# A reworked opening, another order of TensorE's attention work, and values awaited by block, in a two-layer transformer kernel

## What is computed

```python
x = layernorm(x + L0_attn(x))   # energy = x.T @ x (256 x 256), softmax over it, out = x @ attention.T
x = layernorm(x + L0_ffn(x))    # gated FFN, 896 wide, LoRA of 8 experts, top 2 by a router
x = layernorm(x + L1_attn(x))   # causal attention, 16 heads of 16, then w_o
x = layernorm(x + L1_ffn(x))    # 32 experts 96 wide, top 8 cut at a share of 0.8
```

## Time and profile before

| | |
|---|---|
| median of 3 runs | 1439.48 us (1438.6 to 1439.6) |
| the profiled execution's own time | 1448.79 us |
| its span, first to last instruction | 1447.1 us |
| PE busy | 1374.4 us (95%) |
| DVE busy | 931.0 us (64%) |
| ACT busy | 625.9 us (43%) |
| POOL busy | 247.1 us (17%) |
| mean granted TensorE clock | 0.959 of 2.4 GHz |

### The profile page before, as it was taken

How to read it: one execution, slowest core, us unless ns; L and a number is a source line. 1 busy time by engine, 2 the same in 40 slices (tenths; PEclk the granted TensorE clock), 3 DMA queues, 4 the chain that set the end, 5 groups by cost and what they waited for, 6 DMA issues and landing times.

```text
span 1447.1 us, 20119 instructions
## 1 busy us (share of the span) xinstructions
PE 1374.4 (95%) x7836; PEld 975.4 (67%) x7836; DVE 931.0 (64%) x1781; ACT 625.9 (43%) x892; POOL 247.1 (17%) x342
## 2 busy tenths in 40 slices
PE   8999899899899999999999999999999999999996
PEld 6787687687688754344344344454788888888886
DVE  3855754754755777778888888854656455665545
ACT  3323323323323323556666766647343344434432
POOL 1300200200200001022122122211112222222221
PEclk9999999999999985799999999969999999999998
DMA  7000000000000542302201500000011111111110
GB/s 296 1 0 1 0 1 1 0 1 1 22 0 1 163 163 53 77 2 41 49 2 24 67 2 2 13 12 6 19 42 45 46 54 45 44 46 54 44 63 30
DMA packets 32231, 55.40 MB, mean 38 GB/s; under 512 B 6408, under 2 KB 13320, under 8 KB 31752
## 3 DMA queue, kind: packets, MB, share of 16 engines
q1 hardware_dynamic: 30088, 53.85, 13.2%
q0 software_dynamic: 2048, 0.27, 0.1%
HBM read 43.21 MB, written 10.49 MB: 37 GB/s over the span
## 4 chain that ended last, share of the span: by engine, by line
PE 77%; DVE 14%; ACT 4%; issue 3%; DMA 1%; SPq 1%; POOL 0%; POOLq 0%; DVEq 0%; ACTq 0%
PE ps L1393 50%; PE ps L1709 9%; PE ps L1633 9%; PE ps L1687 5%; DVE mpart L1174 4%; ACT probs L833 1%; PE ps L1651 1%; PE ps L1432 1%; SPq L560 1%; DVE x2u L1134 1%; DVE x L914 1%; DMA w_raw<-in_w 1%; PE ps L1718 1%; DVE x2f L1115 1%; DVE x2f L1101 1%
## 5 line engine op out<-in xcount | busy, mean ns | idle before, releaser
L833 ACT ACTIVATE probs<-ps 128x1024 f32<-128x1024 f32 (+3 forms) x320 | 273.7, 895 | 190.4 <-PE ps L1687 189.1
L1393 PE MATMUL ps<-xtd,gu 128*128 128x512 f32 x1152 | 277.9, 395 | 3.6 <-DVE hmul L1301 3.0
L1174 DVE TENSOR_REDUCE mpart<-ps 128x1 f32<-128x512 f32 x384 | 240.1, 683 | 47.0 <-PE ps L1633 45.8
L1393 PEld LDWEIGHTS ps<-xtd,gu 128*128 128x128 f32 x1152 | 212.5, 188 | 52.6 <-issue 4.9
L1633 PE MATMUL ps<-stack 48*128 48x512 f32 (+2 forms) x832 | 206.4, 401 | 16.2 <-DVE mpart L1174 7.7
L1633 PEld LDWEIGHTS ps<-stack 48*128 48x128 f32 x832 | 108.1, 198 | 147.2 <-DVE mpart L1174 92.9
L1393 PE MATMUL ps<-ma,b 128*128 128x512 f32 x672 | 168.8, 400 | 11.2 <-DVE ma L914 7.5
L1687 PE MATMUL ps<-stack 50*128 50x512 f32 (+3 forms) x640 | 161.1, 441 | 8.7 <-ACT probs L833 4.6
L1709 PE MATMUL ps<-probs,vaug 128*32 128x512 f32 (+3 forms) x1280 | 163.6, 587 | 0.7 <-ACT usum L725 0.7
L1393 PEld LDWEIGHTS ps<-ma,b 128*128 128x128 f32 x672 | 126.6, 190 | 43.0 <-DVE ma L914 9.4
L1393 PEld LDWEIGHTS ps<-dn,hpart 128*128 128x128 f32 x1152 | 143.8, 189 | 4.2
(11 more groups left out here) (184 smaller groups left out, 1576.3 us busy)
## 6 DMA issues: line engine op xcount, KB each, us to landing
gu_raw<-in_wgu SPq DMA_DIRECT2D x48, 256.0 KB, 2.6
stack<-qk_dram SPq DMA_DIRECT2D x72, 128.0 KB, 4.0
qk_dram<-qk_out SPq DMA_DIRECT2D x16, 512.0 KB, 2.9
dn_raw<-in_wdn SPq DMA_DIRECT2D x48, 128.0 KB, 2.6
stack<-qk_dram SPq DMA_DIRECT2D x48, 64.0 KB, 2.4
x<-in_x_tm SPq DMA_DIRECT2D x4, 512.0 KB, 5.2
out<-x SPq DMA_DIRECT2D x4, 512.0 KB, 3.1
w_raw<-in_w SPq DMA_DIRECT2D x1, 1792.0 KB, 10.0
```

The source lines that it names most:

```text
L833: act.activation(probs[:, (2 * r + p) % 4, :, off:BLK], banks(bank)[:, :, off:BLK], ACT.Exp, scale=float(HD) ** -0.5).then_inc(exp_done.se ...
L1174: ins = dve.tensor_reduce(part[:, p, qt % TPB, 2 + kb:3 + kb], ps[:, bank, :], AX_X, ALU.max)
L1393: mm = pe.matmul(out, lhs(i), rhs(k), start=first and n == 1, stop=last and n == todo, **more)
```

## The change

Five things change in the opening.

1. PE gets work that nobody reads: `keep_busy(n)` issues n bf16 matmuls of 128x512 into bank 7 from a constant tile of ones that POOL writes first (`const`). Six run ahead of the energy, eight between the energy and the turning of the attention, three between that and the mixing.
2. Tile 0 of `x` has a DMA of its own (`x_first`), ahead of the other four, so that SP issues one DMA more.
3. ACT writes the high part of `w13` in two halves (`w13_hi`); of `a13` only after the exponentials of the energy.
4. DVE subtracts only the first half of `w13` ahead of the maxima; the second half and `a13` come after the copies of `att_t`, ahead of tile 0.
5. `att_t` moves into the place of a quarter of `ma`'s last low part; POOL therefore waits for the last mixing matmul before the third of its four subtractions for block 0.

In the attention `ORDER` is another string, with the same number of each letter, and the wait of `P` for the values moves from all four blocks at once to the block of the round (`v_ready`).

```diff
-    "qqTLRqNqVuuTuuuVuuTuuVMuuuquuquuuquuuSquuuVuuSuuSSuuuPuuPSuuuuSuuuPuuMuuuSuuuuSuuSuSuuuuPuuuuuuuuuuuSSuPuSSPuS"
+    "qqTLRqqNVuTuuVuuuquuqMuTuuuuuSuuSuVuuuPuuSuSuuuquuuVuuPuuMquuSSSuuSPuuuSuuuuuPuuuuuuuuuOuuSuuuSSuuPSSuuuPuuSuS"
...
-        att_t = at("att_t", [P, NC, H], F32, B_END - 11 * BLK * 4)
+        att_t = at("att_t", [P, NC, H], F32, MA + 28 * 1024)
...
+            sp_.dma_start(x[:, 0:1, :], x_tm[:, 0:1, :]).then_inc(x_first, 16)
             for b in range(NB):
-                sp_.dma_start(x[:, TPB * b:TPB * (b + 1), :], x_tm[:, TPB * b:TPB * (b + 1), :]).then_inc(x_in[b], 16)
+                t = max(TPB * b, 1)
+                sp_.dma_start(x[:, t:TPB * (b + 1), :], x_tm[:, t:TPB * (b + 1), :]).then_inc(x_in[b], 16)
...
+            pool.memset(const[:, :], 1.0).then_inc(const_ready, 1)
...
                     pool.wait_ge(*ma_hi.after((b, w, c, 1)))
+                    if (b, w, c) == (0, 1, 0):
+                        pool.wait_ge(*mix_late_ready.after(NT - 1))
...
-            weights_hi("w13", w13_raw, w13)
-            weights_hi("a13", a13_raw, a13)
+            act.wait_ge(w0_in["w13"], 16)
+            for c in range(NC):
+                copy(w13[:, 0, c], w13_raw[:, c]).then_inc(w13_hi, 1)
+            act.wait_ge(w0_in["a13"], 16)
...
+            weights_hi("a13", a13_raw, a13)
             weights_hi("b13", b13_raw, b13)
...
-            weights_lo("w13", w13_raw, w13)
-            weights_lo("a13", a13_raw, a13)
+            def w13_lo(c):
+                dve.wait_ge(w13_hi, c + 1)
+                low(w13[:, 1, c], w13_raw[:, c], w13[:, 0, c]).then_inc(w0_ready["w13"], 1)
+
+            w13_lo(0)
...
                 dve.tensor_copy(att_t[:, j, :], ps[:, 2 + j, 0:H]).then_inc(att_tsb.sem, 1)
+            w13_lo(1)
+            weights_lo("a13", a13_raw, a13)
...
+            pe.wait_ge(const_ready, 1)
+            def keep_busy(n):
+                for i in range(n):
+                    pe.matmul(ps[:, 7, :], const[:, 0:P], const[:, :], start=True, stop=True)
+
+            keep_busy(6)
+            pe.wait_ge(x_first, 16)
...
             pe.wait_ge(consts_in, 80)
+            keep_busy(8)
...
                 mm.then_inc(att_tps.sem, 1)
+            keep_busy(3)
             pe.wait_ge(xfm_in, 16)
...
                         pe.wait_ge(*out0_read.after((NB - 1, TPB - 1)))
-                        pe.wait_ge(*v_ready.after(NB - 1))
+                    if g == 0:
+                        pe.wait_ge(*v_ready.after(qb))
```

More of the change, by code:

```diff
@@ L56 @@
 ORDER = (
[L57 to L66 removed]
+    "qqTLRqqNVuTuuVuuuquuqMuTuuuuuSuuSuVuuuPuuSuSuuuquuuVuuPuuMquuSSSuuSPuuuSuuuuuPuuuuuuuuuOuuSuuuSSuuPSSuuuPuuSuS"
+    "uPuuuuSuMPuuSuSuSuPuuSPuSuSSuuPSuuPuSuSuuPuSuuuuSuPSuuuSuuSuuPuuuSSuuPuSuuuSPuuuSuuPSuuSuuSuuPuuuuPuSuSuuSuSPM"
+    "uuPSuSuSuSPuOSMuSPSuuSuPuuSuSPuuSuSuPuuSSuPSuuuSuPuuSuSPSuuPSSuSuuPuSuSuPSuSPSuMuSuPSuuuSPSuOuSuPuuSuSuPSuPuSu"
+    "uSSuPuuSuOPSuuSuuSuPuSSuPuSuPSuSuuSuMPSuSuuPuSSuuOuPuuuSuPSuuuuSSuPSSuuPuuuSPuuSSuuSPSuuuuSPSuuSuPuSuuPuSSuuSu"
+    "uPuSuuSuPuuSuuPuSuSSuPuSuPuuSSuMPSuuuSuOuPSSuuPuSSuuSuuuPSuuSPuSuuPSMuuSuSuPSuuuPuSuuSuSPuuSuSuMPuuuPuuSSuuSuS"
+    "PSuSuuPuSSuuPuuSSPuSuPuSuuSuuuuSuPSSuuPuuSSuPSSuOPuuuSuuSPSSuuuPOuuSSPSuuuSPSuSMuPuSOuSuPSSuuuuPSuuuuSuyPSuSPu"
+    "SuSuPSuuSuPuYuSSuPuSuSuuPuuuSPuuSuSuuSPuSSuuuPSuuPuSSuuuuuPuSuuSPuMSSuuPuuSuSSuOuPuSSuPuuSSuPuSuSPuuSSuuPuSSuP"
+    "uuSSuPSuuuSPSuSMuPuSuMSPSuSuPSuSuPSuSuOPuuuSSuPSuSuPuSSuuPuSuSuuPuSuuuSuPPuuSuSSuSuPSSuuPuSSuuPuSSPuuuSOPuwSOS"
+    "uuauSPuuSuSPSuPSMuSSuuuPuSuSuuPuSuuSPSuuPuSuuSPuSuOuuSbSPuuSuaSucPPSubSSSuPSuSPuuuSSuPucuSduPSuuSSuPuuSSuPuuSS"
+    "uPuSuuuPuSwdPMeeSOSSaSPSbSrsPSSPSfSPSSPkSSPSSPSSPSSPSSPSSPcSSPmSdPSSSPSxweSP"
 )
@@ L280, in build @@
         assert cursor[0] <= B_END, (cursor[0], B_END)
+        const = at("const", [P, BLK], BF16, B_END + 128)
+        assert cursor[0] <= nc.sbuf_usable_end
         o_tm = at("o_tm", [P, NT, H], F32, R)
@@ L341, in build @@
         xfm_in = sem("xfm_in")
+        x_first = sem("x_first")
+        const_ready = sem("const_ready")
         xlast_in = sem("xlast_in")
@@ L347, in build @@
         pool_const = sem("pool_const")
-        w0_order = ["w13", "a13", "b13", "w2a2", "b2"]
+        w0_order = ["a13", "b13", "w2a2", "b2"]
+        w13_hi = sem("w13_hi")
         w0_hi = sig("w0_hi", w0_order)
@@ L351, in build @@
         pool_step = sem("pool_step")
-        w0_ready = {n: sem(f"w0_ready_{n}") for n in w0_order}
+        w0_ready = {n: sem(f"w0_ready_{n}") for n in ["w13"] + w0_order}
         energy_ready = sig("energy_ready", range(NC))
@@ L1081, in _ @@
             w2a2_lo(0, W2_FIRST)
-            dve.wait_ge(w0_ready["w13"], 1)
+            dve.wait_ge(w0_ready["w13"], NC)
             for b in range(NB):
@@ L1408, in turn_b @@
                     mm.then_inc(turned.sem, 1)
+            pe.wait_ge(const_ready, 1)
[4 more added lines that the diff above has]
+            pe.wait_ge(x_first, 16)
             for t in range(NT):
-                if t % TPB == 0:
+                if t == 1 or t and t % TPB == 0:
                     pe.wait_ge(x_in[t // TPB], 16)
@@ L1548, in _ @@
                 if b == 0:
-                    pe.wait_ge(w0_ready["w13"], 1)
+                    pe.wait_ge(w0_ready["w13"], NC)
                 hidden(0)
```

## The result

The changed kernel took **1467.53 us** (median of 4 runs, 1453.65 to 1483.21), the kernel before 1439.54 us beside it (4 runs, 1438.6 to 1442.39). The ratio is 1.0167 with a 95% interval of 1.0102 to 1.0231: slower, by about 24 us by this ratio, and outside the range of the prediction. (The plain medians are 28 us apart.)

The account below looks back on a forecast made before the run. It took PE to set the pace in the opening and early attention, DVE's maxima nearest the bound from 600 to 945 us. Opening -1.0 and attention -3.5 sum to -4.5: 1439.48 - 4.5 = 1435.0 us, range 1429 to 1443.5.

Parts of the forecast that it names:

- The opening: Up to the first FFN: filled PE, earlier energy and mixing, ln_rstd 1.95 us earlier; taken as -1.0 us (-2.0 to +0.5).
- shorter one: Opening, after PE's idle time: a half-clock stretch half as long as the former 6.9 us, taking 1.7 us of PE's work.
- The moved subtractions: Opening, DVE: 3.2 us at 22.7 to 25.9, not meeting POOL's b13 work; if they met, opening +1.0, share 0.03.
- POOL's new wait: Late mixing ends at 54.65, delaying POOL's third subtraction; fourth ends at 57.2; cost nothing, covered by 1.7 us.
- The wait for the values: Attention: waiting by block costs nothing and alone brings nothing, since all V stood ahead of the first P.
- The named wait of the attention: The eighth q's 1.11 us wait and slow run go, 2.65 us, plus 0.9 from one q moved; attention sum -3.5 us.
- The step that failed: Attention from the 40th unit on: strings same in pace; DVE's idle time could shift 5 us either way, taken as 0.
- slower, by the clock in the attention: Rival: one more half-clock stretch costs 7.2 us, giving 1442.2, or 1443.7 with the opening's gain lost; chance 0.18.
- The price of half clock: Attention, 532 to 600 us: 52 us at half clock lose 7.2 us, by DVE's share falling from 85% to 76%.
- the rival "nothing": Opening +0.5 from halved clock, attention loses only the 1.11 us wait, partly swallowed by DVE: 1438.5; chance 0.26.
- the 32 us more at half clock that "decide": Attention: the slower rival was said to decide from some 32 more us at half clock.
- the 3.63 us: Opening: softmax chain from the first maximum to the mixing's start, added to energy's end 19.1 to give 22.7.

Follow-up runs that it names:

- e1_opening_only: The kernel before with the change's opening alone, old order string and old wait for all values: 1446.96 us, ratio 0.9983.
- i3_values_by_block: The kernel before with only the wait for the values moved to the block of the round, old order: 1438.94 us, ratio 0.9985.
- h1_new_start: The kernel before with the first 151 letters of the new order, old ones after, values awaited by block: 1452.34 us, ratio 1.0007.
- j2_before_burst: The kernel before with 20 filling matmuls in one piece ahead of its 60th unit: 1455.68 us, ratio 1.0091.
- e2_order_only: The kernel before with the new order string and the wait for values by block, old opening: 1463.37 us, ratio 1.0149.
- f1_run_fill: The kernel before with 51 filling matmuls ahead of units at least third in an unbroken run, values awaited by block: 1457.93 us, ratio 1.0083.
- i1_new_middle: The kernel before with letters 152 to 676 of the new order, values awaited by block, old opening: median 1463.38 us, ratio 0.998.

## Why the prediction was wrong, by its own steps

**The opening was right.** The filling ended at 4.12 us (4.2 forecast), the energy at 19.04 (19.1), the mixing started at 22.10 (22.7) and took 8.87 us (8.5), the last step of the variances began at 28.62, early enough to be through before the 30.1 that I gave, but it took 2.66 us beside POOL's `b13`, where it had taken 0.17 before, and ended at 31.28. `ln_rstd` came at 31.42, against 30.95. That is close to the forecast, by a path that it did not have in full: it had POOL's `b13` late and DVE done, and in the trace both end within 0.03 us, with DVE's step stretched beside `b13`; the profile names DVE as what was waited for. The 0.45 us are the extra issue, which delayed `b13` by its upper bound and not by 0.2 us (ACT starts on it at 23.83, before at 23.38). PE idled 2.92 us ahead of the turned block (2.3 forecast), and the clock was at half for 3.4 us, the "shorter one". The moved subtractions did not meet POOL's (`a13` took 1.22 us, as before). POOL's new wait was 3.81 us, ended at 53.88 (54.65), and its cover held: the fourth subtraction ended at 56.46, the product that needs it began at 56.55. By the end of the opening the term was -0.9 us against -1.0. On the whole time it is not seen (e1_opening_only), so the -1.0 in the sum did not come.

**The wait for the values was right**: nothing (i3_values_by_block, 0.9985).

**The named wait of the attention went, but its gain did not come.** The first row below is the seventh `q` of the changed kernel, the second the last one:

```profile
522.92 3.04 PE L1411 MATMUL ps<-xtc,wqkv 128*128 128x512 f32 x12
...
532.64 3.01 PE L1411 MATMUL ps<-xtc,wqkv 128*128 128x512 f32 x12
```

Neither waits, and both run at full clock, where one took 4.57 us after a wait of 1.11. But other waits took its place: up to the 121st maximum PE's waits add up to 5.4 us in the changed kernel and to 4.7 before, and 0.69 us of them are again a wait for DVE's `qk_out`, at 538.02. A block of values met the half clock: 24 matmuls in 5.49 us at 512.81, against 3.13 at 526.55. At the 121st maximum the changed kernel was 4.5 us ahead, just the sum of the prediction (-4.5), and that is luck: it had 18 us less at half clock up to there than the kernel before, worth 6.5 us at 0.361 each. At equal clock the new start is not 3.5 us faster but 1.7 slower (h1_new_start), and the whole new order 2.4 to 4.0.

**The step that failed** is this: "From the 40th unit on the strings are the same in pace, but not in detail, and which PE instruction meets which bank changes. DVE idles 53 us from 600 to 945; a tenth of it either way is 5 us. I take 0." DVE's idle time there went from 53 to 73 us (345 - 272.17), and not by banks but by the clock. By the fit, the 24 us by which the changed kernel's mean lies over that of all 81 runs before are 2.4 us at equal clock and 0.361 x (165 - 104) = 22 us of clock. So the step that was put at nothing, for the lack of a difference in pace, holds nearly the whole loss. The right rival was "slower, by the clock in the attention"; it had the place ("if the new order thins PE's work elsewhere so that one more such stretch comes"), but too small a chance and too small a price.

**The price of half clock was mis-sized.** I took 7.2 us for 52 us, 0.14 for each, from DVE's share in two windows of different work. Measured are 0.361 over all runs, and in the stretch from 835.70 to 873.20, by DVE's progress at the same place in both kernels, 37.5 x (31.62 - 20.94) / 31.62 = 12.7 us, 0.34 for each. The same order at both clocks gives 0.31 (the 121st to the 161st maximum, above). In these stretches PE has hardly a gap (36.83 us of 37.50), and DVE follows at PE's pace. With 0.36 the rival would have stood at 1435 + 19 = 1454 us for one more stretch like that of 532 to 600.

Some of the prediction's smaller sums are off too, and none of them changes the outcome: by its own terms the rival "nothing" comes to 1438.9 and not 1438.5; with the opening's gain lost the slower rival comes to 1443.2 and not 1443.7; the 32 us more at half clock that "decide" only bring its sum back to 1439.5, and at 0.14 each it takes 53 to reach 1442.4; and the 3.63 us were counted from DVE's first maximum, 0.32 us behind the energy's end, so that the mixing would follow at 23.0.

The Trainium skill (TensorE: Matmul & The Clock Gate, Terms) prices such time at (1 - K/N), which makes an estimate of 0.5 of a us for each at half clock. The measured 0.361 is below it, and three things are seen that lower it. A P of eight goes from 1.06 to 1.93 us, which is 0.45 for each us at half clock. The 20 us of 345 in which PE idles at full clock do not grow with it. And in some places DVE is the bound even at half clock, as in this window of j2_before_burst's profile, ahead of its piece, with DVE busy 15.77 of 16.20 us:

```profile
539.60:555.80 16.20, 15.71 (x45) 7.98 (x44) 15.77 (x30) 3.30 (x5) 2.87 (x6) 0.50 0.14 34
```

Whether these make up the whole difference no run shows. The rule was much nearer than my rows' 0.14, and it was not used.

**The spread was too narrow.** Three runs within 1 us were taken as the kernel's own spread. Its real one is 36 us wide, and nearly all of that is time at half clock (60 to 158 us in the 81 runs). The eight runs with the new `ORDER` and no filling, of the changed kernel and of e2_order_only, have 119 to 205 us, 155 on average.

**What stays open** is what in the letters lets the clock fall and what ends a fall. Filling ahead of long runs of units did not help (f1_run_fill), and the last part of the string alone does not do it, though one of the two long falls lies there. That identical programs differ by up to 167 us at half clock (i1_new_middle, 63 to 230) says that something besides the letters decides it too. No run here tests what.

## What to carry to other kernels

Where a kernel's clock falls and comes back in a stretch in which PE and another engine are both near the bound, read the time at half clock of *many* runs first, and split every comparison into a constant and a price times that time; three runs that agree say nothing of the spread. Price a us at half clock by the same work at both clocks (here 0.31 to 0.36), not by windows with different work. An order of work that differs in hundreds of places is not "the same in pace": if nothing bounds its effect on the clock, the range has to hold one long stretch more and one less.
